# One recurrence in a language-model kernel: the state update as 32-row products of one batch each, the state copied in one piece, the correction term moved to GpSimd

## The reference, cut to what matters

```python
def step(carry, inp):
    W1c, b1c = carry
    q, k, v, e = inp
    Z1 = jnp.einsum('bhkd,bhde->bhke', k, W1c) + b1c
    grad = ln_l2_bwd(Z1, v - k, ttt_norm_scale, ttt_norm_bias)
    ...
    last_e = e[..., -1, :, None]
    W1n = W1c - jnp.einsum('bhkd,bhke->bhde', last_e * k, grad)
    b1n = b1c - jnp.sum(last_e * grad, axis=-2, keepdims=True)
    ...
def ln_l2_bwd(x, target, g, b):
    ...
    xh = (x - mu) / std
    gx = (xh * g + b - target) * g
    return (gx - gx.mean(-1, keepdims=True) - xh * (gx * xh).mean(-1, keepdims=True)) / std
```

## Time and profile before

| | us |
|---|---|
| median of 3 runs (1444.8 to 1446.53) | 1444.83 |
| profiled execution, its own time | 1442.97 |
| profiled execution, span | 1441.2 |
| TensorE busy in the span | 1295.5 |
| VectorE busy | 919.8 |
| ScalarE busy | 709.2 |
| GpSimd busy | 377.0 |
| mean granted TensorE clock | 0.955 |

### The profile page before, as it was taken

One profiled execution on the slowest core, in us unless ns is written; L12 is line 12 of the kernel. 1 busy time (PEld: TensorE's weight loads), 2 busy tenths in 40 slices (PEclk: granted clock), 3 DMA queues, 4 the chain that ended last, 5 costly groups with the idle time before them and its releaser, 6 DMA issues. The chain is left out here.

```text
span 1441.2 us, 29234 instructions
## 1 busy us (share of the span) xinstructions
PE 1295.5 (90%) x11395; PEld 874.1 (61%) x11395; DVE 919.8 (64%) x2227; ACT 709.2 (49%) x1512; POOL 377.0 (26%) x428
## 2 busy tenths in 40 slices
PE   4899999799869999889999998889887788799999
PEld 3432333356537777567777776777664344388888
DVE  6568887423557777499888878887875787500011
ACT  1426555432124443488888874767654233343410
POOL 6400000000047777355666650000000333300000
PEclk9979999869979999899999999999998999999999
DMA  3432121000132334444343452212103100067721
GB/s 94 115 104 61 51 61 30 26 0 1 37 96 90 102 118 133 154 123 126 104 131 101 140 133 60 56 39 61 40 1 131 80 1 0 1 236 289 272 96 45
DMA packets 99285, 127.42 MB, mean 88 GB/s; under 512 B 24589, under 2 KB 87804, under 8 KB 94956
## 3 DMA queue, kind: packets, MB, share of 16 engines
q1 hardware_dynamic: 97612, 123.96, 27.8%
q0 software_dynamic: 1536, 1.59, 0.4%
HBM read 89.06 MB, written 37.88 MB: 88 GB/s over the span
## 5 line engine op out<-in xcount | busy, mean ns | idle before, releaser
L637 DVE TENSOR_REDUCE mx<-bank 128x1 f32<-128x512 f32 x192 | 119.7, 681 | 18.5 <-PE bank L559 18.2
L697 ACT ACTIVATE PT<-bank 128x1024 f32<-128x1024 f32 x96 | 94.3, 1022 | 69.7 <-PE bank L575 69.1
L1729 POOL TENSOR_SCALAR r_grD<-gr 32x192 f32<-32x192 f32 x192 | 101.8, 530 | 101.4 <-DVE gr L1623 56.0
L1460 PE MATMUL bank<-r_grD,ek 128*128 128x256 f32 x384 | 100.9, 399 | 0.0
L2455 DVE TENSOR_TENSOR eo_all<-bank,m_b2s 128x768 f32<-128x768 f32 x8 | 7.7, 958 | 142.3 <-PE bank L2416 142.3
L2447 ACT ACTIVATE x_g<-bank,m_b1s 128x128 f32<-128x128 f32 x192 | 51.4, 400 | 75.7 <-PE bank L2398 75.7
L1460 PEld LDWEIGHTS bank<-r_grD,ek 128*128 128x128 f32 x384 | 68.3, 191 | 9.5
L559 PE MATMUL bank<-K,Q 97*128 97x512 bf16 x192 | 68.9, 411 | 5.1 <-DVE mx L637 3.3
L2331 POOL TENSOR_SCALAR m_xs<-m_xs 128x256 f32<-128x256 f32 x4 | 2.5, 631 | 259.7 <-DVE m_xs L2235 258.6
L1673 ACT ACTIVATE r_t<-r_xh,r_cd 128x64 f32<-128x64 f32 x192 | 70.0, 427 | 0.7
L1451 PEld LDWEIGHTS bank<-gr,r_A 128*128 128x128 f32 x384 | 48.3, 193 | 34.2 <-DVE gr L1623 32.0
(11 more groups left out here) (366 smaller groups left out, 3206.4 us busy)
## 6 DMA issues: line engine op xcount, KB each, us to landing
wb<-in_m_w SPq DMA_DIRECT2D x32, 1152.0 KB, 6.0
k_d<-p_krows SPq DMA_DIRECT2D x48, 256.0 KB, 2.8
ek<-k_d SPq DMA_DIRECT2D x32, 384.0 KB
tgt<-c_d SPq DMA_DIRECT2D x33, 196.0 KB
c_d<-p_rows SPq DMA_DIRECT2D x32, 196.0 KB, 2.9
g_d<-gr SPq DMA_DIRECT2D x32, 192.0 KB
o_G<-g_d SPq DMA_DIRECT2D x32, 192.0 KB, 3.0
qk_d<-a_parts SPq DMA_DIRECT2D x24, 192.0 KB, 3.1
```

Source lines behind the costliest of these rows:

```text
L637: v.tensor_reduce(mx[u % 2][:, j // 4, j % 4:j % 4 + 1], slot(f"A{u}.{j}"), AX.X, ALU.max).then_inc(*dve.did(f"max{u}.{j}"))
L697: a.activation(PT[kt % 2][:, 2 * hp:2 * hp + 2, :], STB[s % 2][:, :, :], ACT.Exp, scale=DH ** -0.5)\
L1460: last = t_.matmul(SP_[g][:, i * B * E1:(i + 1) * B * E1], ek[r][:, p, :], grD[g][:, i, :, :].rearrange("p b e -> p (b e)"), start=False, ...
L1729: last = g_.tensor_scalar(grD[g][rr, :, b, :], b3(gr[j % RING][rr, cols(g)]), 0.0, None, ALU.bypass)
```

## The change

It does five things. (1) `grD` is gone, with the three GpSimd instructions and the ScalarE one that wrote it. (2) The state lies in PSUM by batch, one bank for each batch with both groups in it (`held`), and `into_state` makes 12 products a half step, each with 32 rows of one batch, on four row groups of the array; `into_bias` makes four products of 48 columns in place of one of 192. (3) ScalarE copies the state in one instruction of 960 columns. (4) The three instructions `t` and the product `rl` run on GpSimd. (5) TensorE updates the state right behind `into_z`, behind the copy of the other group, and `before` comes ahead of `spread`; VectorE computes `var` ahead of `red`. The layout of the stored state in DRAM follows, and each of its tiles is loaded with four transfers in place of two.

```diff
+        SC, BC = (WC + GC) // B, GC // B
+        by_b = lambda ap: ap.rearrange("p (b c) -> p b c", b=B)
...
-        grD = [sb(f"r_grD{g}", [P, GP, B, E1]) for g in range(G)]
...
-        SP_ = [M["ps2"][g].rearrange("p a n -> p (a n)") for g in range(G)]
+        held = lambda g: M["ps8"][:, 0:B, g * SC:(g + 1) * SC]
...
-        dve = Steps(sem("r_dve"), per("u0", "gx0", "pr0", "red0", "var1", "cd0", "rs1", "rl1", "xh1", "g0",
-                                      "u1", "gx1", "pr1", "red1", "var0", "cd1", "rs0", "rl0", "xh0", "g1"))
-        act = Steps(sem("r_act"), per("A0", "sq1", "std1", "t0.0", "t0.1", "t0.2", "S1", "d0", "A1", "sq0", "std0", "t1.0", "t1.1", "t1.2", "S0", "d1"))
-        pe = Steps(sem("r_pe"), per("Z0", "pre1", "X0", "ua0", "upd0", "Z1", "pre0", "X1", "ua1", "upd1"))
-        pool = Steps(sem("r_pool"), per("d0", "kz0", "d1", "kz1"))
+        dve = Steps(sem("r_dve"), per("u0", "gx0", "pr0", "var1", "red0", "cd0", "rs1", "xh1", "g0",
+                                      "u1", "gx1", "pr1", "var0", "red1", "cd1", "rs0", "xh0", "g1"))
+        act = Steps(sem("r_act"), per("A0", "sq1", "std1", "S1", "A1", "sq0", "std0", "S0"))
+        pe = Steps(sem("r_pe"), per("Z0", "upd0", "pre1", "X0", "Z1", "upd1", "pre0", "X1"))
+        pool = Steps(sem("r_pool"), per("t0.0", "t0.1", "t0.2", "rl1", "kz0", "t1.0", "t1.1", "t1.2", "rl0", "kz1"))
...
-                    sp.dma_start(M["W_d"][sc, :, g * GP:(g + 1) * GP].rearrange("p h b e -> p (h b e)"), state_of(sc * SPT, g)[:, 0:WC])\
-                        .then_inc(snapped[g], 16)
-                    sp.dma_start(M["B_d"][sc, :, cols(g)], state_of(sc * SPT, g)[:, WC:WC + GC]).then_inc(snapped[g], 16)
+                    state = by_b(state_of(sc * SPT, g))
+                    sp.dma_start(M["W_d"][sc, :, g], state[:, :, 0:GC]).then_inc(snapped[g], 16)
+                    sp.dma_start(M["B_d"][sc, :, cols(g)].rearrange("p (b c) -> p b c", b=B), state[:, :, GC:SC]).then_inc(snapped[g], 16)
...
-                            sp.dma_start(O["Wd"][t][rr, :, rr], M["W_d"][t, rr, :, 0, :]).then_inc(O["tiles_in"][t], 16)
+                            for g in range(G):
+                                sp.dma_start(O["Wd"][t][rr, g * GP:(g + 1) * GP, rr],
+                                             M["W_d"][t, rr, g, 0, :].rearrange("p (h e) -> p h e", e=E1)).then_inc(O["tiles_in"][t], 16)
...
-                    t_.matmul(SP_[g][:, WC:WC + GC], lastb[:, :], gr[r][:, cols(g)], start=False, stop=False, skip_group_check=True)
-
-                def into_state(g, r, part):
-                    for i, p in list(enumerate(heads(g)))[part]:
-                        last = t_.matmul(SP_[g][:, i * B * E1:(i + 1) * B * E1], ek[r][:, p, :], grD[g][:, i, :, :].rearrange("p b e -> p (b e)"),
-                                         start=False, stop=False, skip_group_check=True)
+                    for b in range(B):
+                        t_.matmul(held(g)[:, b, GC:SC], lastb[:, :], by_b(gr[r][:, cols(g)])[:, b, :], start=False, stop=False,
+                                  skip_group_check=True)
+
+                def into_state(g, r):
+                    for i, p in enumerate(heads(g)):
+                        for b in range(B):
+                            rr = slice(32 * b, 32 * b + 32)
+                            last = t_.matmul(held(g)[:, b, i * E1:(i + 1) * E1], ek[r][rr, p, :], gr[r][rr, p * E1:(p + 1) * E1],
+                                             start=False, stop=False, skip_group_check=True)
...
                         t_.wait_ge(*dve.at(f"g0.{j}", sc))
                         t_.wait_ge(*act.at(f"A0.{j}", sc))
                         into_z(0, r).then_inc(*pe.did(f"Z0.{j}"))
+                        t_.wait_ge(*act.at(f"S1.{j}", sc))
+                        t_.wait_ge(ek_in[r], 16 * (sc * (SPT // RING) + j // RING + 1))
                         into_bias(0, r)
-                        t_.wait_ge(*act.at(f"S1.{j}", sc))
+                        into_state(0, r).then_inc(*pe.did(f"upd0.{j}"))
                         t_.wait_ge(*dve.at(f"xh1.{j}", sc))
                         t_.wait_ge(*ago(pool, "kz1", j, 2, sc))
                         bias(1, sc * SPT + j)
+                        before(1, (j + 1) % KR, sc * SPT + j).then_inc(*pe.did(f"pre1.{j}"))
                         spread(0)
-                        before(1, (j + 1) % KR, sc * SPT + j).then_inc(*pe.did(f"pre1.{j}"))
                         t_.wait_ge(*ago(pool, "kz1", j, 1, sc))
                         gram(0, (j + 1) % KR).then_inc(*pe.did(f"X0.{j}"))
-                        t_.wait_ge(ek_in[r], 16 * (sc * (SPT // RING) + j // RING + 1))
-                        t_.wait_ge(*pool.at(f"d0.{j}", sc))
-                        t_.wait_ge(*act.at(f"d0.{j}", sc))
-                        into_state(0, r, slice(0, 2)).then_inc(*pe.did(f"ua0.{j}"))
-                        into_state(0, r, slice(2, 3)).then_inc(*pe.did(f"upd0.{j}"))
...
+                        v.wait_ge(tgt_in[r], 16 * (sc * (SPT // RING) + j // RING + 1))
...
+                        v.wait_ge(*act.at(f"sq{o}.{j}", sc))
+                        variance(o).then_inc(*others("var"))
...
-                        v.wait_ge(*act.at(f"sq{o}.{j}", sc))
-                        variance(o).then_inc(*others("var"))
...
+                        if g:
+                            v.wait_ge(*pool.at(f"rl1.{j}", sc))
+                        else:
+                            v.wait_ge(*ago(pool, "rl0", j, 1, sc))
...
-                        if g:
-                            m = sc * (SPT // RING) + (j + 1) // RING + 1
-                            v.wait_ge(tgt_in[rn], 16 * m)
-                        else:
-                            v.wait_ge(tgt_in[rn], 16 * (sc * (SPT // RING) + j // RING + 1))
...
-                        rates(o, rn).then_inc(*others("rl"))
...
-                            v.wait_ge(*act.at(f"t{g}.{i}.{j}", sc))
+                            v.wait_ge(*pool.at(f"t{g}.{i}.{j}", sc))
...
-                        a.wait_ge(*dve.at(f"cd{g}.{j}", sc))
-                        for i in range(GP):
-                            c = slice(i * E1, (i + 1) * E1)
-                            a.activation(t1[g][:, c], xh[g][:, c], ACT.Identity, bias=cd[g][:, 0, i:i + 1], scale=cd[g][:, 1, i:i + 1])\
-                                .then_inc(*act.did(f"t{g}.{i}.{j}"))
...
-                        a.wait_ge(*(pe.at(f"ua0.{j}", sc) if g else ago(pe, "ua1", j, 1, sc)))
-                        a.activation(state_of(to, o)[:, 0:PART], SP_[o][:, 0:PART], ACT.Copy)
...
-                        a.activation(state_of(to, o)[:, PART:WC + GC], SP_[o][:, PART:WC + GC], ACT.Copy).then_inc(*act.did(f"S{o}.{j}"))
-                        a.wait_ge(*dve.at(f"g{g}.{j}", sc))
-                        a.wait_ge(*ago(pe, f"upd{g}", j, 1, sc))
-                        for b in (3,):
-                            rr = slice(32 * b, 32 * b + 32)
-                            last = a.activation(grD[g][rr, :, b, :], b3(gr[j % RING][rr, cols(g)]), ACT.Copy)
-                        last.then_inc(*act.did(f"d{g}.{j}"))
+                        a.activation(by_b(state_of(to, o)), held(o), ACT.Copy).then_inc(*act.did(f"S{o}.{j}"))
...
-                            g_.wait_ge(*dve.at(f"g{g}.{j}", sc))
-                            g_.wait_ge(*ago(pe, f"upd{g}", j, 1, sc))
-                            g_.wait_ge(*(pool.at(f"kz0.{j}", sc) if g else ago(pool, "kz1", j, 1, sc)))
+                            o = 1 - g
+                            turn, rn = sc * (SPT // RING) + (j + g) // RING + 1, (j + g) % RING
...
-                            for b in (0, 1, 2):
-                                rr = slice(32 * b, 32 * b + 32)
-                                last = g_.tensor_scalar(grD[g][rr, :, b, :], b3(gr[j % RING][rr, cols(g)]), 0.0, None, ALU.bypass)
-                            last.then_inc(*pool.did(f"d{g}.{j}"))
+                            g_.wait_ge(*(pool.at(f"kz0.{j}", sc) if g else ago(pool, "kz1", j, 1, sc)))
+                            g_.wait_ge(*dve.at(f"cd{g}.{j}", sc))
+                            for i in range(GP):
+                                c = slice(i * E1, (i + 1) * E1)
+                                g_.tensor_scalar(t1[g][:, c], xh[g][:, c], cd[g][:, 1, i:i + 1], cd[g][:, 0, i:i + 1], ALU.mult, ALU.add)\
+                                    .then_inc(*pool.did(f"t{g}.{i}.{j}"))
+                            g_.wait_ge(*dve.at(f"rs{o}.{j}", sc))
+                            g_.wait_ge(tgt_in[rn], 16 * turn)
+                            g_.tensor_tensor(rl[o][:, :], rs[o][:, :], tgt[rn][:, HALF + o * GP:HALF + (o + 1) * GP], ALU.mult)\
+                                .then_inc(*pool.did(f"rl{o}.{j}"))
+                            g_.wait_ge(*pool.at(f"rl{o}.{j}", sc))
...
-                            g_.wait_ge(*pool.at(f"d{g}.{j}", sc))
```

(8 more changed lines are left out.)

46 lines of the change are left out of this document (20 added, 26 removed).

## The result

| | before | changed |
|---|---|---|
| median of 4 runs each, us | 1444.82 | 1651.0 (1649.34 to 1653.17) |
| profiled execution, us | 1442.97 | 1653.17 |
| mean granted clock of TensorE | 0.955 | 0.817 |

The changed kernel takes 1.1447 times as long (95% interval 1.1418 to 1.1477). The prediction had 1454 us, at most 1486.

What follows compares the result with a forecast made beforehand. The VectorE and `t` chain bounded the half step at 3.94 us, TensorE would at 4.10: 9.8 - 1.5 + 0.9 + 0.2 = +9.4 us, 1442.97 to 1452.4, median 1454 us; range 1445 to 1486.

Steps and rivals of the forecast that it cites:

- the two half steps at a granted clock of about half: Recurrence, 602 to 610 us: TensorE's extra 0.47 us counts double there, a term of +0.9 us.
- a granted clock that falls below 1.00 behind 610 us: Recurrence: a sign of being wrong, making every TensorE step longer; no size given.
- TensorE's half step: Recurrence: TensorE's own work per half step was to go from 3.63 to 4.10 us.
- The chain: Recurrence, VectorE and `t` on GpSimd until `gr` reaches TensorE: 3.87 to 4.00 us, just below TensorE's 4.10.
- The whole sum: Whole kernel: +9.4 us, from 1442.97 to 1452.4 us for the profiled execution.
- Row groups overlap only in pairs: `into_state`: takes 1.42 us instead of 0.71, half step 4.81, +53 us, 1498 us; chance 0.14.
- The estimate of 0.86: `into_state`: priced by the skill's 3.07 times, 0.15 us more than in the sum, the kernel some 9 us more.
- Faster: `into_bias`: loads of the same weights cost 0.04 us each, `into_bias` 0.5 shorter; 1432 or 1424 us; chance 0.13.
- GpSimd sets the pace: Recurrence: `gr` and `t` hold each other up at the shared memory port; chain 4.32, 1469 us, or 1488; chance 0.20.
- No change: Recurrence: same relief on TensorE but `t` at 1.09, chain 3.87 to 4.00 against 3.94; about 1445 us; chance 0.05.
- its 0.18 us: VectorE's `pr`: 0.54 us beside GpSimd's copies, 0.36 where GpSimd was idle; the difference may return.
- The state copy: ScalarE's one copy of 960 columns: below 1.02 us, ending before 3.7, with 1 us of cover before TensorE wants it.

Runs made afterwards that it cites:

- e1: The changed kernel with 14 unread identity products ahead of the recurrence and 16 behind the state update in each of the first eight half steps: 1470.14 us.
- e5: The changed kernel with 14 unread identity products ahead of the recurrence and none in the half steps: 1449.52 us.
- e7: The kernel of e1 with some 6 us of VectorE work between steps 15 and 16, for which TensorE waits: 1580.93 us.
- e10: The kernel before with some 6 us of VectorE work at step 16, for which TensorE waits: 1449.63 us.
- h1: The changed kernel with each 32-row state product streaming 192 columns instead of 64: 1477.13 us, ratio 1.0235 to the kernel before.
- e6_first: The changed kernel with 16 unread identity products behind each of the first two state updates and none ahead: 1461.14 us, ratio 1.0144 to the kernel before.
- h5: The changed kernel with one 192-column bias product, 14 unread products ahead and 16 in each of the first two half steps: ratio 1.0051 to the kernel before.
- h6: The kernel of h5 with `t` and its place in the order back on ScalarE: ratio 0.9948 to the kernel before.
- e3: The changed kernel with three state products of 128 rows and 192 columns instead of twelve on row groups: 1451.74 us.
- e4: The changed kernel with `spread` back ahead of `before`: 1476.77 us in its first run.
- h4: The kernel of e4 again, in four further executions: 1461.69 to 1480.76 us, ratio 1.0184 to the kernel before.
- e11: The kernel of e5 with `t` back on ScalarE: 1453.38, 1456.6, 1643.42 and 1647.07 us in four executions.

## Why the prediction was wrong

**The step that failed** is in the sum: it gives a lower clock only to "the two half steps at a granted clock of about half" and prices all others at 1.00, from rows 1, which are of the kernel before. The last sentence named "a granted clock that falls below 1.00 behind 610 us" as what would prove it wrong, without a rival, a price or a chance. Its term of +0.9 us should have been 61 x (7.30 - 4.10) = 195 us. What I took for a property of the time in the program was one of what TensorE does there: the old half step, with state products of 256 columns, took the clock back within some 10 us of its fall, the new one, with 64, doesn't. That follows from e1, e5 and e7 (at 1.00 the new half step stays there, at 0.50 it stays as well), e10 (the old one recovers from the same wait), and h1 (the new one recovers too once its state products are long). The Trainium skill, "TensorE: Matmul & The Clock Gate", "Part 1: The HAM clock gate", says that sustained activity releases the engine from the 1.2 GHz level. Here the trace disagrees: TensorE had records over 450 of 450 us at 0.50. If the clock had come back, the time would be e6_first's or e5_ahead's, 1449 to 1461 us.

**What was right, seen at the full clock (e1_warm).** TensorE's half step: 4.10 predicted, 4.10 measured. By steps, each with the change behind it: `into_z` 0.71 (0.71 in the sum), `into_bias` 0.98 (0.97), `into_state` 0.82 (0.81), `bias` 0.53 (0.52), `before` 0.47 (0.47), `spread` 0.27 (0.26 to 0.34), `gram` 0.32 (0.30). The chain: `gr` ends at 746.84, 3.91 us behind `into_z` (3.87 to 4.00). The whole sum agrees with e5_ahead, as far as one execution can tell: 12.4 us above the kernel before on its chip, against 9.4. In the chain some luck helped: `cd` took 0.17 us and not 0.28, and GpSimd began 0.17 behind it and not 0.08.

**The rivals.**
- *Row groups overlap only in pairs*: fell. 24 passes took 0.82 - 0.09 = 0.73 us, so four groups with 64 columns lose almost nothing against 0.71. With 192 columns (h1) they took 1.10 against 1.07 by the same prices. The estimate of 0.86 from the Trainium skill's 3.07 ("TensorE: Matmul & The Clock Gate", "Measured speedup vs the span model", where the products have 512 columns) is too long for them.
- *Faster* (loads of the same weights shrink): fell. Eight bias passes took 0.88, that is 0.11 each.
- *GpSimd sets the pace*: fell. At the full clock TensorE is the later one, as forecast: `gr` lies ready for 0.19 us (e1, 746.84 to 747.03). Where TensorE is out of the way the chain is 4.03 us (h5), just above the 3.87 to 4.00 and far from 4.32. Three `t` took 1.13 us at least, mostly 1.19 and up to 1.60 in early half steps, not 1.09; a lone one 0.40 and not 0.32. `gr` on VectorE and `t` on GpSimd run side by side: in e1 the first `gr` (745.89, 0.34 us, against 0.28 in the kernel before) lies over the second `t` (745.77, 0.39 us), which is no longer than the first.
- *No change*: fell. TensorE's 4.10 stands above the chain's 3.91 in e1.
- `pr` got its 0.18 us back (0.36 now), but `gx` takes 0.54 beside the `key` copy (0.36 in h6, where they don't meet), which itself went from 0.84 to 1.04: the contention moved to a neighbour.
- The state copy took 0.97 us (at most 1.02), under its cover.

**Open.** h1 and e3 show that longer state products are enough to bring the clock back, 10 to 20 us behind its fall. They don't show that it needs them: with the old order of `spread` and `before` (e4, h4) it comes back with 64 columns too, some 65 us into the recurrence in both profiles, and the extra products of 128 columns did so in e6. Which quality of TensorE's work decides isn't shown. So "at 0.50 it stays" holds for the changed half step as it is, in the four executions of the changed kernel by their mean clocks (0.817 to 0.823) and in e7. Why single executions of e11 (two of four), h5, h6 and e6 lose the clock, or get it back late, is open too; in h5's profile it went in the half step behind a wait of 0.74 us for `gr`.

## What to carry to other kernels

The granted clock that a profile shows for a stretch holds for the work that TensorE did in it, and not for another kernel's work in its place: when a change rewrites the products of a stretch, look in the profile for where the clock falls and what brought it back before, and give "it doesn't come back" a price and a chance of its own; here that was 195 us beside 9. Cutting wide products into many narrow ones may take away what brought it back, even where TensorE's sum at the full clock comes out right to a hundredth. If a wait ahead of a loop is what costs the clock, a few idle products in the wait (14 here, 1651 to 1450 us in the one execution of e5) can bring it through. That isn't safe: with the same 14 products two of e11's four executions took 1643 and 1647 us, and one later stall undid it in e7. And when a chain moves to another engine, price how late that engine begins, not only how long it works.
